# Two more steps with Q by seven half products, and the combinations they need made earlier

## The chip, the cores and the metric

The kernel runs on one core of a Trainium2 chip. The metric is the device time of one execution in microseconds, the median of several runs.

## The reference

A cross-attention layer with a gate, then a quantized linear layer with a gate. `x` and the context are (32, 64, 512); there are 32 heads in 8 groups of 4 that share K and V, and head size is 128.

```python
Q = (layernorm(x) @ Wq.T).reshape(b, s, 8, 4, 128)
K = (ctx @ Wk.T).reshape(b, s, 8, 128)
V = (ctx @ Wv.T).reshape(b, s, 8, 128)
scores = einsum('bqhed,bkhd->bheqk', Q, K) * 128 ** -0.5      # causal mask
probs = softmax(scores)
attn = einsum('bheqk,bkhd->bqhed', probs, V).reshape(b, s, 4096)
x = x + tanh(g_xattn) * (attn @ Wd.T)
x = x + tanh(g_ffn) * (layernorm(x) @ dequantized.T + bias)
```

## The kernel before, in words

**Numbers in two halves.** Every float32 operand of a large product is scaled by a power of two and written as a high and a low float16 part. ScalarE (ACT) writes the high part, VectorE (DVE) or GpSimd (POOL) the low one, and TensorE (PE) multiplies high by high, high by low and low by high (`PASSES`). So one product over 512 inputs of 512 columns is 12 matmuls, each 128x512.

**Steps.** The 2048 tokens are 4 blocks of 512. A step n handles one group of heads g = n % 8 of one block tb = n // 8, so there are 32 steps. In step n PE computes the scores of n, then Q, K and V of the next step m = n + 1, transposes the probabilities of n, multiplies them by V (`av_unit`), and adds the output product of n (`y_unit`, four units, one for each tile of 128 tokens, with the weight `wd`). The order on every engine is written out by hand, and semaphores tie the engines together. In block 0 the weights are read in float32, split and kept in DRAM (`kept_q`, `kept_k`, `kept_v`, `kept_d`); from block 1 on each step reads its split weights back (`back_qkv` at line 431, `back_d` at line 445), all from SyncE's queue (SP), which issues its DMAs strictly in the order of the program.

**Q by seven half products.** For a step m with `fast(m)` Q is not made by `q_unit` but by `run` (line 1741). For two heads at a time the product of weights and tokens is cut in two along the heads, the inputs and the tokens, and the eight quarter products are replaced by seven (Strassen's scheme in Winograd's form). A half product is 6 matmuls of 128x256; two pairs of heads make 14 of them, 84 matmuls, in place of 48 of 128x512. ACT copies partial results out of PSUM (`copy_p1`, `copy_p5`, `copy_u2`), DVE adds others to them, and both split the sums into the halves of q. Before the change `FIRST_FAST` is 24, so steps 24 to 31 are fast, all of block 3.

**What a fast step needs beforehand.** The sums of quarters of the weights ("mixed" weights) of each group, made once: `load_mix` reads a group's float32 weights into `raw_s` (half of `raw_d`), POOL combines them (`mix_weights`, four operations), ACT and DVE split them (`mix_hi`, `mix_lo`) into `ws`, and `keep_mix` writes them to `kept_s`. `MIX_STEPS` says in which steps this happens, one group each; `back_mix` reads them back for a fast step, issued two steps ahead. The tokens need combinations too: `mix_norm` makes them from the normalised block on POOL, with `mixed_hi` on ACT and `mixed_lo` on POOL, in the step with g = 4 of the block before (`mix_of`); `transpose_mixed` turns them by 32 DMA transposes into `tT`, which lies in `raw_q`, 16 each in two steps.

**Put-off output units.** When the step after next is fast (`deferred(n)` is `fast(n + 2)`), y units 2 and 3 of step n run in the middle of step n + 1. In a step whose successor is fast, `back_d(n)` waits for them, since they still read the buffer of `wd`, so `transpose_some` (line 499) issues it behind the first `FEW` = 5 of the step's transposes and not ahead of all of them:

```python
for one in some:
    ...
    if one is some[FEW - 1] and fast(n + 1) and n < LAST:
        back_d(n)
```

The norm of a block comes in step 3 of the block before, its transposes in the steps after it; in step 20 these are 18. Step 10 unpacks half of the FFN weight on DVE (`ffn_weight`) and takes the norm's statistics; step 11 has the FFN of block 0 among its matmuls.

Of the kernel before, what the change touches and what calls it, by code (L numbers as in the profile page):

```python
# [15 lines left out]
HEADS, GROUPS, DK = 32, 8, 128  # L16
HPG = HEADS // GROUPS
KC = D // P
# [37 lines left out]
def build(nc, x, ctxT, wqT, wkT, wvT, wdT, g_x, g_f, qw, w_scale, w_zero, bias, out):  # L56
    with ExitStack() as stack:
        def sb(name, shape, dt=F32):
            return stack.enter_context(nc.sbuf_tensor(name, shape, dt))
# [4 lines left out]
        def sem(name):  # L64
            return stack.enter_context(nc.semaphore(name))
# [11 lines left out]
        raw_q = sb("raw_q", [P, 2, HPG, KC, DK])  # L77
# [3 lines left out]
        raw_d = sb("raw_d", [P, 2, HPG, D])  # L81
# [5 lines left out]
        k = sb("k", [P, 2, BT], F16)  # L87
# [7 lines left out]


        tT = [raw[:, 0, :, :, :].rearrange("p h k n -> p (h k n)").bitcast(F16).rearrange(
            "p (c k n) -> p c k n", c=2, k=KC) for raw in (raw_q, raw_q)]
        ws = [raw[:, 1, :, :, :].rearrange("p h k n -> p (h k n)").bitcast(F16).rearrange(
            "p (c h k n) -> p c h k n", c=2, h=HPG, k=KC)  # L100
            for raw in (raw_q, raw_d.rearrange("p c h (k n) -> p c h k n", k=KC))]
# [63 lines left out]
        def pair(name):  # L165
            return [sem(name + "0"), sem(name + "1")]
# [5 lines left out]
        s_ld, s_kept, s_back = sem("s_ld"), pair("s_kept"), pair("s_back")  # L172
        s_mix, s_hi, s_lo = sem("s_mix"), sem("s_hi"), sem("s_lo")
# [18 lines left out]
        wq_hi, wq_lo = sem("wq_hi"), sem("wq_lo")  # L192
# [35 lines left out]
        def backs(m):  # L228

            return 16 * ((m - GROUPS) // 2 + 1)  # L230
# [71 lines left out]

        FIRST_FAST = 3 * GROUPS
        FIRST_BLOCK = FIRST_FAST // GROUPS
        RUN = ((0, 1), (0, 5), (0, 2), (0, 6), (0, 7), (0, 3), (1, 1), (1, 5), (1, 2), (1, 6), (1, 7), (1, 3))

        def fast(m):

            return FIRST_FAST <= m < STEPS

        def pair_count(m, r):

            return 2 * (m - FIRST_FAST) + r + 1

        def run_count(m, r, i):

            return len(RUN) * (m - FIRST_FAST) + RUN.index((r, i)) + 1

# [17 lines left out]
            return part.rearrange("p (b u s) -> p b u s", b=BPB // 2, u=HALVES)  # L338


        MIX_STEPS = (7, 12, 13, 14, 15, 17, 18, 21)
        MIX_ORDER = tuple((FIRST_FAST + i) % GROUPS for i in range(GROUPS))

        def mixing(n):

            return MIX_STEPS.index(n) if n in MIX_STEPS else None

# [38 lines left out]
        def _(sp):  # L386
# [101 lines left out]

            def transpose_mixed(tb, some):

                sp.wait_ge(wq_lo, HPG * GROUPS)
                for t, c, i in some:
                    sp.wait_ge(t_hi, TILES * (tb - FIRST_BLOCK) + t + 1)
                    sp.wait_ge(t_lo, TILES * (tb - FIRST_BLOCK) + t + 1)
                    sp.dma_start(tT[tb % 2][:, c, i, t * P:(t + 1) * P], th[:, t, c, i * P:(i + 1) * P],
                                 transpose=True).then_inc(t12_ld if t >= 2 else t3_ld if i < 2 else t4_ld, 16)


            def transpose_some(n):

                g, tb = n % GROUPS, n // GROUPS
                some = []
                if tb > 0 and g in (1, 2):
                    call = NORMS.index((2, tb - 1))
                    some = transposes(call)[16 * (g - 1):16 * g]
                elif 0 < tb < BLOCKS - 1 and g >= 4:
                    call = NORMS.index((1, tb + 1))
                    if fast(GROUPS * (tb + 1)):
                        if g == 4:
                            some = transposes(call)[EARLY:]  # L510
                        elif g < 7:
                            call, some = None, MIXED[16 * (g - 5):16 * (g - 4)]
                    elif g < 6:
                        some = transposes(call)[16 * (g - 4):16 * (g - 3)]
                    elif tb + 1 >= FIRST_BLOCK:
                        call, some = None, MIXED[16 * (g - 6):16 * (g - 5)]
                for one in some:
                    if call is None:
                        transpose_mixed(tb + 1, [one])
                    else:  # L520
                        transpose_norm(call, [one])
                    if one is some[FEW - 1] and fast(n + 1) and n < LAST:
                        back_d(n)
                if not some and fast(n + 1) and n < LAST:
                    back_d(n)
# [23 lines left out]
            def back_mix(m):  # L549

                sp.wait_ge(q_mm, 4 * (m - 1))
                sp.wait_ge(s_kept[m % 2], 16 * GROUPS // 2)
                sp.dma_start(ws[m % 2].rearrange("p c h k n -> p (c h k n)"), kept_s[m % GROUPS]).then_inc(s_back[m % 2], 16)

            def load_ffn():
# [36 lines left out]
            for n in range(STEPS):  # L592
                g, tb, m = n % GROUPS, n // GROUPS, n + 1
# [18 lines left out]
                if fast(m + 1):  # L612
                    back_mix(m + 1)
# [1094 lines left out]
        def _(pe):  # L1708
# [32 lines left out]
            def run(m, r, i):  # L1741
# [3 lines left out]
                if (r, i) == (0, 1):  # L1745
                    pe.wait_ge(q_back[m % 2], backs(m))
                    pe.wait_ge(s_back[m % 2], 16 * ((m - FIRST_FAST) // 2 + 1))
                    if m % GROUPS == 0:
# [417 lines left out]
```

## Time and profile before

| | us |
|---|---|
| median of 3 runs | 1046.54 (1046.34 to 1047.17) |
| profiled execution | 1045.23 |
| its span, first to last instruction | 1043.4 |
| PE busy | 1006.0 |
| DVE busy | 720.3 |
| ACT busy | 500.3 |
| POOL busy | 290.2 |
| mean granted clock of TensorE | 0.997 of 2.4 GHz |

Busy time is the union of an engine's instructions. The timeline gives instructions in order of time, with equal neighbours merged; a start is counted from the first instruction of the span. A step is taken to begin with the first matmul of its scores. Line numbers are those of the kernel before.

### The profile page before, as it was taken

The page shows a single profiled execution, that of the slowest core. Times are in us where ns is not written, and L with a number is a line of the kernel's source. Part 1 is how long each engine was busy: PE and PEld are TensorE (multiplying, and loading weights), DVE is VectorE, ACT ScalarE, POOL GpSimd, SP SyncE. Part 2 cuts the span into 40 slices and gives each one's busy share as a digit, 9 for nine tenths or more (in the row PEclk, how much of TensorE's full clock was granted, in tenths as well). Part 3 has the DMA queues.
Part 4 walks back from the last instruction along what each step waited for, and adds up shares of the span by engine and source line. Part 5 has one row for each costly group of instructions (what it writes and reads, how often), then busy time and mean ns, then how long its engine had stood idle before and what let it go on. Part 6 is the DMA issues. An engine that isn't in the chain of part 4 may idle for free.

```text
span 1043.4 us, 21305 instructions
## 1 busy us (share of the span) xinstructions
PE 1006.0 (96%) x8130; PEld 597.5 (57%) x8130; DVE 720.3 (69%) x1484; ACT 500.3 (48%) x1033; POOL 290.2 (28%) x287
## 2 busy tenths in 40 slices
PE   5889999999999999999999999999999999999996
PEld 3455555555555555455555555555567776767752
DVE  6856777777586676865667667565667767666678
ACT  5777676675633343334543434334444444444422
POOL 1355665465714001412210503143000120000004
PEclk9999999999999999999999999999999999999998
DMA  7748546534474542455544775146754444543211
GB/s 281 229 150 289 204 160 203 163 101 169 130 258 139 155 92 102 157 157 177 207 172 162 237 212 176 26 162 181 216 162 149 158 130 148 180 140 138 91 42 60
DMA packets 97523, 168.65 MB, mean 162 GB/s; under 512 B 35472, under 2 KB 68240, under 8 KB 83728
## 3 DMA queue, kind: packets, MB, share of 16 engines
q1 hardware_dynamic: 97424, 167.30, 49.6%
q8 instruction: 66, 1.08, 0.5%
q14 instruction: 33, 0.27, 0.1%
HBM read 110.89 MB, written 33.55 MB: 138 GB/s over the span
## 4 chain that ended last, share of the span: by engine, by line
PE 84%; DVE 10%; ACT 3%; issue 2%; DMA 1%; SPq 0%; DVEq 0%; ACTq 0%
PE pa L1715 33%; PE py L1715 30%; PE av L1894 5%; PE pa L1790 4%; PE av L1790 3%; PE pp L1872 3%; PE ps L1856 2%; PE pp L1856 2%; DVE q L1214 2%; PE py L1954 1%; DVE sc L1310 1%; DVE row_max L1308 1%; DVE sc L1304 1%; DVE sc L1321 1%; DMA raw_q<-in_wqT 1%
## 5 line engine op out<-in xcount | busy, mean ns | idle before, releaser
L1715 PE MATMUL py<-wd,att 128*128 128x512 f16 x1488 | 337.6, 379 | 1.7 <-DVE att L1334 0.9
L1715 PE MATMUL pa<-xT,wq 128*128 128x512 f16 x1152 | 257.2, 379 | 10.1 <-DVE q L1214 7.8
L1715 PEld LDWEIGHTS py<-wd,att 128*128 128x128 f16 x1488 | 143.1, 98 | 158.6 <-issue 2.8
L1715 PEld LDWEIGHTS pa<-xT,wq 128*128 128x128 f16 x1152 | 109.3, 98 | 145.2 <-issue 19.3
L1343 DVE SCALAR_TENSOR_TENSOR xacc<-py,f_y,xacc 128x512 f32<-128x512 f32 x128 | 95.7, 747 | 91.4 <-PE py L1715 91.3
L939 ACT ACTIVATE att<-av 128x256 f16<-128x256 f32 x256 | 80.8, 385 | 135.9 <-PE av L1894 135.4
L1334 DVE SCALAR_TENSOR_TENSOR att<-av,att 128x256 f16<-128x256 f32 x256 | 93.5, 418 | 65.6 <-ACT att L939 65.3
L888 ACT ACTIVATE q<-pa 128x512 f16<-128x512 f32 x96 | 56.7, 591 | 171.0 <-PE pa L1715 171.0
L1715 PE MATMUL pa<-wv,cT 128*128 128x128 f16 x1536 | 96.2, 219 | 0.0
L1715 PEld LDWEIGHTS pa<-wv,cT 128*128 128x128 f16 x1536 | 89.8, 98 | 0.9
L1214 DVE SCALAR_TENSOR_TENSOR q<-pa,q 128x512 f16<-128x512 f32 x96 | 65.8, 686 | 35.2 <-ACT q L888 33.5
L1715 PE MATMUL pa<-cT,wk 128*128 128x512 f16 x384 | 88.1, 379 | 1.6 <-DVE q L1214 1.4
L1894 PE MATMUL av<-pT,v_dup 128*128 128x256 f16 x512 | 71.6, 273 | 0.1
L680 POOL TENSOR_TENSOR xh<-xn,xh 128x512 f16<-128x512 f32 x28 | 33.8, 1234 | 124.0 <-ACT xh L912 124.0
L928 ACT CAST pr<-sc 128x256 f16<-128x256 f32 x64 | 32.7, 510 | 74.2 <-DVE sc L1321 74.1
L1214 DVE SCALAR_TENSOR_TENSOR k<-pa,k 128x512 f16<-128x512 f32 x32 | 22.1, 692 | 65.9 <-ACT k L894 65.9
L932 ACT COPY pT<-pp 128x1024 f16<-128x1024 f16 x64 | 64.3, 1005 | 4.7 <-PE pp L1872 4.2
L657 POOL TENSOR_SCALAR raw_d<-raw_d,w_mul 128x512 f32<-128x512 f32 x32 | 54.2, 1693 | 21.9 <-ACT wd L883 21.9
L1715 PEld LDWEIGHTS pa<-cT,wk 128*128 128x128 f16 x384 | 36.4, 98 | 41.7 <-issue 3.2
L747 POOL TENSOR_TENSOR xacc<-xacc,raw_kv 128x512 f32<-128x512 f32 x12 | 17.1, 1447 | 154.7 <-DVE raw_kv L1483 154.7
L1894 PEld LDWEIGHTS av<-pT,v_dup 128*128 128x128 f16 x512 | 48.2, 99 | 16.7 <-issue 0.3
L697 POOL TENSOR_TENSOR small<-rs 128x4 f32<-128x4 f32 x18 | 4.7, 262 | 168.4 <-DVE rs L1368 167.4
(180 smaller groups left out, 1396.8 us busy)
## 6 DMA issues: line engine op xcount, KB each, us to landing
wq<-kept_q SPq DMA_DIRECT2D x24, 1024.0 KB, 8.7
wd<-kept_d SPq DMA_DIRECT2D x23, 1024.0 KB, 6.8
v_dup<-v_nat SPq DMA_DIRECT2D x128, 128.0 KB, 2.4
raw_d<-in_wdT SPq DMA_DIRECT2D x8, 1024.0 KB, 10.3
kept_q<-wq SPq DMA_DIRECT2D x8, 1024.0 KB, 9.0
kept_d<-wd SPq DMA_DIRECT2D x8, 1024.0 KB, 5.6
raw_d<-in_wqT SPq DMA_DIRECT2D x8, 1024.0 KB, 7.1
raw_q<-in_wqT SPq DMA_DIRECT2D x7, 1024.0 KB, 5.5
```

Source lines behind the costliest of these rows:

```text
L657: pool.tensor_scalar(raw, raw, scale, None, ALU.mult).then_inc(w_scaled, 1)
L680: pool.tensor_tensor(xh[:, t % TILES, LO, :], xn[:, t % TILES, :], xh[:, t % TILES, HI, :], ALU.subtract).then_inc(x_lo, 1)
L888: act.activation(q[:, HI, :, :, h, :], pa[h % 2][:, :].rearrange("p (b u s) -> p b u s", b=BPB, u=HALVES), ACT.Copy, scale=Q_SCALE).then_i ...
L932: act.copy(pT[:, :, :, p * HQ:(p + 1) * HQ], pp[:, :].bitcast(F16).rearrange("p (b h s) -> p b h s", b=BPB, h=HPG)).then_inc(pT_ok, 1)
L939: last = act.activation(att[:, HI, :, at:at + S], av[j % 2][:, bb * 256:(bb + 1) * 256].rearrange("p (h s) -> p h s", h=HPG), ACT.Copy, sc ...
L1214: dve.scalar_tensor_tensor(out=out, in0=in0, scalar=scale, in1=hi, op0=ALU.mult, op1=ALU.subtract).then_inc(done, 1)
L1334: last = dve.scalar_tensor_tensor(out=att[:, LO, :, at:at + S], in0=av[j % 2][:, bb * 256:(bb + 1) * 256].rearrange("p (h s) -> p h s", h= ...
L1343: dve.scalar_tensor_tensor(out=acc(t), in0=py[j % 2][:, :], scalar=f_y[:, n:n + 1], in1=acc(t), op0=ALU.mult, op1=ALU.add).then_inc(y_ok, 1)
L1715: last = pe.matmul(out, stationary(a, i), moving(b, i), start=(i == 0 and (a, b) == PASSES[0]), stop=(i == count - 1 and (a, b) == PASSES[ ...
L1790: last = pe.matmul(half(bank), a[:, c, head, w_half + kc, :], b[:, d, b_half + kc, at], start=first and i in (1, 2, 5), stop=kc == 1 and ( ...
L1856: last = pe.matmul((pp, ps)[p][:, b * keys(p):(b + 1) * keys(p)], q[:, a, b, p, :, :].rearrange("p h s -> p (h s)"), k[:, c, b * S:b * S + ...
L1894: last = pe.matmul(av[j % 2][:, bb * 256:(bb + 1) * 256], v_dup[:, n % 2, b, c, :], pT[:, b, :, :].rearrange("p h s -> p (h s)"), start=(c ...
```

## The change

`FIRST_FAST` goes from 24 to 22. Steps 22 and 23, groups 6 and 7 of block 2, so get their Q by half products too, and their Q is made during steps 21 and 22. From this follow, by the rules above:

- `deferred` holds for steps 20 and 21 as well, and `fast(n + 1)` for n = 21 and 22: `back_d` of these two moves behind five transposes.
- `back_mix` of steps 22 and 23 is added to SP's queue, in steps 20 and 21, 1 MB each.
- `FIRST_BLOCK` becomes 2, so the combinations of block 2's tokens are made too: `mix_norm`, `mixed_hi` and `mixed_lo` in step 12, 32 more DMA transposes in steps 14 and 15.
- The order of the groups that are mixed begins with 6 and 7, and `MIX_STEPS` has 10 in place of 21. Step 12 mixes weights next to the norm's combinations. The first read of mixed weights waits for all of them.
- The transposed combinations of block 3 lie in `raw_d`, no longer in `raw_q`, and so wait for the last mixing of weights.

```diff
-            "p (c k n) -> p c k n", c=2, k=KC) for raw in (raw_q, raw_q)]
+            "p (c k n) -> p c k n", c=2, k=KC) for raw in (raw_q, raw_d.rearrange("p c h (k n) -> p c h k n", k=KC))]
...
-        FIRST_FAST = 3 * GROUPS
+        FIRST_FAST = 2 * GROUPS + 6
...
-        MIX_STEPS = (7, 12, 13, 14, 15, 17, 18, 21)
+        MIX_STEPS = (7, 10, 12, 13, 14, 15, 17, 18)
...
             def transpose_mixed(tb, some):
 
-                sp.wait_ge(wq_lo, HPG * GROUPS)
+                if tb == 2:
+                    sp.wait_ge(wq_lo, HPG * GROUPS)
+                else:
+                    sp.wait_ge(s_lo, HPG * GROUPS)
...
             def back_mix(m):
 
                 sp.wait_ge(q_mm, 4 * (m - 1))
-                sp.wait_ge(s_kept[m % 2], 16 * GROUPS // 2)
+                for par in range(2):
+                    sp.wait_ge(s_kept[par], 16 * GROUPS // 2)
```

SP's queue from the end of step 20 to step 21, before (`xT<-xh` are the norm's transposes, `raw_q<-raw_kv` those of the combinations, `raw_d<-in_wqT` the raw weights for the mixing of step 21):

```order
L486 DMA_TRANSPOSE xT<-xh 128x128 x18
L462 DMA v_dup<-v_nat 64x4x256 x4
L541 DMA raw_d<-in_wqT 128x2048
L449 DMA wd<-kept_d 128x4096
L436 DMA wq<-kept_q 128x4096
L440 DMA wk<-kept_k 128x1024
L443 DMA wv<-kept_v 128x1024
L495 DMA_TRANSPOSE raw_q<-raw_kv 128x128 x16
```

and now (`<-kept_s` are loads of mixed weights):

```order
L557 DMA raw_q<-kept_s 128x4096
L486 DMA_TRANSPOSE xT<-xh 128x128 x18
L462 DMA v_dup<-v_nat 64x4x256 x4
L436 DMA wq<-kept_q 128x4096
L440 DMA wk<-kept_k 128x1024
L443 DMA wv<-kept_v 128x1024
L557 DMA raw_d<-kept_s 128x4096
L498 DMA_TRANSPOSE raw_d<-raw_kv 128x128 x5
L449 DMA wd<-kept_d 128x4096
L498 DMA_TRANSPOSE raw_d<-raw_kv 128x128 x11
```

The load of wd has moved from ahead of wq's to behind five transposes; a load of mixed weights stands ahead of the 18 transposes and another ahead of the five.

PE at the end of step 20 and in the first part of step 21, before:

```order
L1715 MATMUL py<-wd,att 128x512 x12
L1894 MATMUL av<-pT,v_dup 128x256 x4
L1715 MATMUL py<-wd,att 128x512 x24
L1856 MATMUL pp<-k,q 128x32 x24
L1856 MATMUL ps<-k,q 128x64 x24
L1715 MATMUL pa<-xT,wq 128x512 x48
```

and now:

```order
L1719 MATMUL py<-wd,att 128x512 x12
L1898 MATMUL av<-pT,v_dup 128x256 x4
L1860 MATMUL pp<-k,q 128x32 x24
L1860 MATMUL ps<-k,q 128x64 x24
L1794 MATMUL pa<-xT,wq 128x256 x6
L1794 MATMUL pa<-raw_q 128x256 x6
L1794 MATMUL av<-xT,wq 128x256 x6
L1794 MATMUL pa<-raw_q 128x256 x6
L1719 MATMUL py<-wd,att 128x512 x12
```

Two y units (x24) have left the end of step 20; the first of them stands behind four half products of step 21.

## Rows read from the trace of the kernel before

**Rows 1.** The page, part 1: PE's busy time.
```profile
PE 1006.0 (96%) x8130; PEld 597.5 (57%) x8130; DVE 720.3 (69%) x1484; ACT 500.3 (48%) x1033; POOL 290.2 (28%) x287
```

**Rows 2.** Busy time by step (20 to 23, 25, 26): stretch, length, engines, clock, DMA.
```profile
677.62:708.21 30.59, 30.21 (x237) 16.95 (x236) 18.52 (x33) 11.73 (x24) 16.05 (x14) 1.00 0.45 143
708.21:738.48 30.27, 30.21 (x237) 16.93 (x236) 19.29 (x36) 14.54 (x28) 8.03 (x7) 1.00 0.56 160
738.48:763.58 25.10, 25.04 (x214) 14.60 (x213) 14.72 (x29) 11.44 (x22) 2.31 (x2) 1.00 0.76 226
763.58:792.44 28.86, 28.86 (x274) 20.52 (x272) 19.51 (x44) 12.46 (x30) 0.00 (x0) 1.00 0.54 175
...
821.63:850.50 28.87, 28.87 (x275) 20.54 (x273) 19.42 (x44) 14.90 (x38) 7.12 (x6) 1.00 0.42 143
850.50:880.33 29.83, 28.90 (x275) 20.53 (x273) 21.40 (x47) 12.46 (x30) 2.54 (x3) 1.00 0.52 160
```

**Rows 3.** Timeline of PE in step 25: start, length, engine, line, operation.
```profile
832.73 2.75 PE L1715 MATMUL py<-wd,att 128*128 128x512 f16 x12
...
844.45 2.75 PE L1715 MATMUL py<-wd,att 128*128 128x512 f16 x12
```

**Rows 4.** Timeline of SP's queue in steps 20 and 21.
```profile
688.24 23.23 SPq L486 DMA_TRANSPOSE xT<-xh  x18
711.57 2.60 SPq L462 DMA_DIRECT2D v_dup<-v_nat  x4
...
715.40 0.38 SPq L436 DMA_DIRECT2D wq<-kept_q  x1
...
717.18 22.11 SPq L495 DMA_TRANSPOSE raw_q<-raw_kv  x16
```

**Rows 5.** Timeline of SP's queue in step 26.
```profile
855.43 0.55 SPq L436 DMA_DIRECT2D wq<-kept_q  x1
...
857.04 0.59 SPq L553 DMA_DIRECT2D raw_q<-kept_s  x1
857.74 6.28 SPq L486 DMA_TRANSPOSE xT<-xh  x5
864.38 0.33 SPq L449 DMA_DIRECT2D wd<-kept_d  x1
```

**Rows 6.** Line L449, wd's loads: all 23, then that of step 26 alone.
```profile
DMA to landing us min/median/max: 4.7/6.8/10.1
...
DMA to landing us min/median/max: 7.2/7.2/7.2
```

**Rows 7.** Line L1471 in all; timelines of POOL, PE and DVE in step 12.
```profile
L1471 DVE SCALAR_TENSOR_TENSOR xacc<-ff_rows,small,xacc x16: 742/782/1748, 423.0 to 1037.5; 128x512 f32<-128x512 f32 x16
...
429.77 5.58 POOL L747 TENSOR_TENSOR xacc<-xacc,raw_kv 128x512 f32<-128x512 f32 x4
...
437.68 2.75 PE L1715 MATMUL pa<-xT,wq 128*128 128x512 f16 x12 [0.66 <-DVE q L1214]
...
455.05 1.41 DVE L1214 SCALAR_TENSOR_TENSOR raw_d<-raw_d,w_mul 128x512 f16<-128x512 f32 x2
```

**Rows 8.** Timeline of ACT at the end of step 20 and in step 23.
```profile
703.78 2.18 ACT L1000 ACTIVATE raw_kv<-xn 128x512 f16<-128x512 f32 x4
...
765.73 0.37 ACT L948 COPY p<-pa 128x256 f32<-128x256 f32 x1 [1.30 <-PE pa L1790]
```

**Rows 9.** Timelines of DVE and PE in step 11.
```profile
395.52 0.68 DVE L1214 SCALAR_TENSOR_TENSOR q<-pa,q 128x512 f16<-128x512 f32 x1
...
398.67 2.75 PE L1715 MATMUL pa<-xT,wq 128*128 128x512 f16 x12
```

**Rows 10.** PE's timeline in the tail, then a stretch of it with its granted clock.
```profile
1024.32 3.63 PE L1954 MATMUL py<-ff_w,xT 128*128 128x512 f16 x16 [0.66 <-ACT xT L919]
...
1030.88 5.31 PE L1954 MATMUL py<-ff_w,xT 128*128 128x512 f16 x16 [0.49 <-DVE xn L1483]
...
1031.20:1034.50 3.30, 3.30 (x10) 1.09 (x9) 3.27 (x5) 0.55 (x1) 3.30 (x3) 0.50 0.00 0
```

## The prediction, made before the run

> **What bounds the kernel now.** I read the page first: TensorE is busy 1006.0 of 1043.4 us, 96% [rows 1]. So I cut the span into steps at the first score matmul of each step and read busy times by step [rows 2]. Step 21 lasts 30.27 us with PE busy for 30.21, step 25, which makes its Q by half products, 28.87 with PE busy for all of it. Every other engine has at least 9 us left over in such a step. The rule that follows: a step takes what its matmuls take, and another engine or a transfer matters only where PE arrives and finds its operand missing. So the change is priced in two ways: matmuls removed, and new places where PE can arrive too early.
>
> **What it removes.** Steps 21 and 22 compute the Q of groups 6 and 7 of block 2. Each becomes a step like 25: 30.27 - 28.87 = 1.40 us less. Step 22 is short in the trace before (25.10) only because y units 2 and 3 of its output product are put off into step 23. Now step 20 puts off its two first, steps 21 and 22 hand two on and take two, step 23 is as it was. Steps 20 to 23 together go from 30.59 + 30.27 + 25.10 + 28.86 = 114.82 to 25.41 + 28.87 + 28.87 + 28.86 = 112.01. **Term 1: -2.8 us.** The important by-product: step 21 no longer starts at 708.21 but at 677.62 + 25.41 = 703.03, 5.2 us sooner, because its predecessor gave work away.
>
> **What it adds on the SP queue of step 21; this decides.** SP issues in order, and it is late there already: step 20's 18 transposes hold it from 688.24 to 711.57, then come four copies of V, then the loads of step 21 [rows 4]. None of this waits for PE, so it does not move up with PE. I write SP's new clock:
> - A load of mixed weights (1 MB) stands ahead of the 18 transposes. Such a load holds SP 0.6 us [rows 5]. The V copies end at 711.57 + 2.60 + 0.6 = 714.8.
> - The load of raw weights for the mixing of step 21 and wd's load go from here. The wq, wk, wv loads take 717.18 - 715.40 = 1.8, the second new load of mixed weights 0.7: 717.3.
> - Now the change's own order: wd's load stands behind five transposes, since its buffer is free only once the put-off y units have run. Five hold SP 22.11 / 16 x 5 = 6.9 [rows 4] or 6.3 [rows 5]. I take 6.6: wd is issued at 723.9.
> - wd lands 7.2 us after its issue in step 26, the nearest case, with the same loads and transposes ahead of it [rows 5, 6]: 731.1. Over all steps it is 4.7 to 10.1, median 6.8 [rows 6].
>
> When does PE want it? In step 25, y unit 0 starts 844.45 - 821.63 = 22.8 us into the step [rows 3], so at 703.03 + 22.8 = 725.8, or 726.1 with the small wait below. **Term 2: 731.1 - 726.1 = +5.0 us of PE standing still.** Bounds: five transposes at 6.3 and a landing in 4.7 give 2.2 us; 6.9 and 10.1 give 8.2. The buffer itself is no limit: the second put-off y unit starts 832.73 - 821.63 = 11.1 into the step [rows 3] and ends 2.7 later, at 717, while SP gets there at 723.9.
>
> In step 22 the same order is harmless. That step then starts near 737; SP is through with the 11 other transposes (15.2) and the V copies near 742, 5 us into the step, as in step 26 (850.50 to 880.33), where SP began its loads at 855.43 and wd, issued at 864.38, landed at 871.6, ahead of the 873.3 at which it was wanted [rows 2, 5, 6]. Term: 0, up to 1.
>
> **What the wait does to the clock.** The tail shows what an idle PE costs: after a stretch with waits the granted clock reads 0.50, the 1.2 GHz level, and the 16 matmuls that took 3.63 us at the full 2.4 GHz take 5.31 [rows 10], 1.68 more. I expect the clock to fall once during or after the 5 us; part of the slow stretch may fall into the wait itself, where it is free. Ends 0 and 1.7, I take 1.1. **Term 3: +1.1.** The Trainium skill (TensorE: Matmul & The Clock Gate, the section on HAM oscillation) says the same of PE gaps spent waiting for a DMA: it comes back at half rate. By its rule the term is nearer to the full 1.7 than to 0; nothing in the middle of this trace tests it, since PE never waits there for over 1 us.
>
> **Mixing of weights, moved from step 21 to step 10.** Step 21 had room for it. Step 10 has the tightest DVE: behind y unit 1 stand the norm's statistics and the unpacking of the FFN weight, and DVE does the first low part of q in step 11 only at 395.52 [rows 9]. Four low parts more are 2 x 1.32 = 2.6 us (two take 1.41, overlapping by a little [rows 7]), so that part moves to 398.2 and ends at 398.8. PE wants it at 398.67, after the first FFN tile. Step 11's FFN units give DVE its time back. **Term 4: +0.3**, between 0 and 1.5 (if the unpacked weight is late as well).
>
> **Norm's combinations in step 12.** POOL gets eight operations more, some 11 us at the 1.4 us that four of its additions took apiece [rows 7], right behind the mixing of weights, so beside DVE's four low parts. Where POOL's additions overlapped, one DVE operation on SBUF operands (L1471) took up to 1.75 us in place of 0.74, and PE lost 0.66 at its fourth Q unit of step 12 [rows 7]. The same can happen in step 13. **Term 5: +0.5**, between 0 and 1.5. The Trainium skill (GPSIMD Engine Reference, its quick facts) has POOL and DVE contend for one SBUF interface when DVE reads two SBUF tensors; the low parts are of that kind. By that rule all four stretch and the term is at its upper end; were there no such contention, it would be 0. The 32 new transposes of steps 14 and 15 take SP 22 of 30.27 us in each, as in steps 12 and 13, where nothing waited: 0, or a few tenths. ACT's new hi parts fill idle time.
>
> **Start of step 21.** ACT does the norm's hi parts for block 3 until 703.78 + 2.18 = 706.0. Nobody wanted ACT then; now step 21 needs its first copy, in step 23 made 2.15 us after the start (765.73) [rows 8], so at 705.2. It comes 0.8 later; PE uses it after a few half products more. DVE's scores meet POOL there too. **Term 6: +0.3**, between 0 and 1.
>
> **Sum:** -2.8 + 5.0 + 1.1 + 0.3 + 0.5 + 0.3 = +4.4. The profiled execution took 1045.23 us and would take 1049.6; the median of the runs is 1046.54, 1.3 above it, so I forecast **1050.9**.
>
> **Rivals.**
> - *A, wd's load comes in time.* The other side: faster. Place: SP in step 21. It decides at an issue before 726.1 - 7.2 = 718.9. For it: in steps 25 and 26 this very order costs nothing [rows 5, 6]. Against it: there SP was idle ahead of it, here it is 5 us behind from step 20. Also if transposes issue quicker with their sources long ready. Time: -2.8 + 0.8 on 1046.5, about 1044.7. Chance 0.13.
> - *B, a short wait, no loss of clock.* wd lands in 4.9 and SP is a little quicker: 2.5 us, small terms 0.8. Time 1047. Chance 0.2. For it: the loads of step 21 stand in a queue with fewer bytes, since raw weights and a write of mixed weights are gone.
> - *C, more than one wait.* SP's delay carries into step 22 (wd again) or DVE falls behind in steps 13 and 21 by their upper ends: 1054. Chance 0.12. For it: the wq, wk, wv and mixed loads pile up with 16 transposes. Against: the 5 us wait itself gives SP time.
> - *D, the change misses its aim:* half products that run where PE waits for DVE and save nothing. Steps 23 and 25 ran at 28.86 and 28.87 [rows 2], so I give this no chance of its own; step 26 (29.83) shows what a DVE with four operations more does, and that is inside C.
>
> **How the numbers follow.** The main case has 0.55: a wait of 4 to 6 us, with or without the clock, 1049 to 1053. The range takes in all of it, B, part of A and most of C: 1044.8 to 1054.5. A measurement of this kernel tells 0.2% (2.1 us) from nothing. Slower than that: the main case but its lower edge (0.53) and C (0.12), 0.65. Within: B and that edge, 0.23. Faster by more: A at its best, 0.12.
>
> **What would show it.** A PE wait of about 5 us ahead of y unit 0 of step 21, ended by the load of wd, which SP issued near 724 behind five transposes; a granted clock of 0.50 just after it. Steps 20 to 23 otherwise near 25.4, 28.9, 28.9, 28.9. A wait of some tenths at the third Q unit of step 11 and in step 13. I am wrong if wd's load of step 21 is issued before 719, or lands within 4 us, or if step 22 shows the larger wait. If the total comes out right with step 21 at 29 us, it was right by accident.

## The result, and the profile after

The changed kernel takes 1051.79 us in the median of five runs (1049.03 to 1054.55), the kernel before 1046.34 beside it. The ratio is 1.0050, 95% interval 1.0037 to 1.0064: **slower by 5.2 us, between 3.9 and 6.7**. A later series on another occasion gave 1.0044 (1.0030 to 1.0058). The profiled execution took 1051.79 too, its span is 1050.0.

Busy time by step in the profile after, steps 20 to 23 (answers to [rows 2]); the columns are the stretch, its length, then PE, PEld, DVE, ACT, POOL, the granted clock, DMA:

```profile
679.98:705.39 25.41, 25.04 (x213) 14.59 (x212) 16.48 (x30) 9.00 (x18) 12.32 (x10) 1.00 0.70 207
705.39:741.37 35.98, 31.28 (x275) 21.06 (x273) 19.58 (x43) 16.77 (x38) 7.50 (x6) 0.91 0.48 139
741.37:770.23 28.86, 28.86 (x274) 20.55 (x272) 18.91 (x43) 14.92 (x34) 2.32 (x2) 1.00 0.52 165
770.23:799.09 28.86, 28.86 (x274) 20.54 (x272) 19.49 (x44) 12.47 (x30) 0.00 (x0) 1.00 0.51 166
```

Three of the four are what the half products promise. Step 21 is 7.1 us too long, and it alone shows a clock below 1.00. Its place is in PE's timeline:

```profile
732.94 5.12 PE L1719 MATMUL py<-wd,att 128*128 128x512 f16 x12 [4.70 <-DMA wd<-kept_d]
...
738.34 2.75 PE L1719 MATMUL py<-wd,att 128*128 128x512 f16 x12
```

That is y unit 0 of step 21. PE stood for 4.70 us until the load of wd landed; then its 12 matmuls took 5.12 us, those of the next unit 2.75. SP's queue (answers to [rows 4, 5]):

```profile
690.90 24.34 SPq L486 DMA_TRANSPOSE xT<-xh  x18
715.34 2.60 SPq L462 DMA_DIRECT2D v_dup<-v_nat  x4
718.05 0.55 SPq L436 DMA_DIRECT2D wq<-kept_q  x1
...
719.67 0.58 SPq L557 DMA_DIRECT2D raw_d<-kept_s  x1
720.35 6.27 SPq L498 DMA_TRANSPOSE raw_d<-raw_kv  x5
726.72 0.53 SPq L449 DMA_DIRECT2D wd<-kept_d  x1
```

The load of wd was issued at 726.72, 21.3 us into the step, and landed 6.2 us later:

```profile
DMA to landing us min/median/max: 6.2/6.2/6.2
```

The granted clock around it, in two stretches of the same columns as above (answers to [rows 10]):

```profile
728.20:730.90 2.70, 0.04 (x1) 0.00 (x0) 1.10 (x3) 2.62 (x5) 0.73 (x1) 1.00 0.84 328
731.00:737.70 6.70, 4.76 (x12) 1.73 (x13) 0.00 (x0) 0.32 (x1) 1.48 (x2) 0.50 0.19 43
```

PE had been idle since 728.2; the clock fell to 0.50 (1.2 GHz) within the wait and stayed there until PE had worked 4.8 us again. By length, step 21 is 28.87 + 4.70 + 2.41, and the last number is the clock.

Steps 11 and 12 (answers to [rows 7, 9]) show the work that moved forward. They took 37.33 and 30.88 before:

```profile
392.83:430.48 37.65, 37.55 (x274) 20.38 (x273) 28.97 (x64) 11.85 (x24) 8.55 (x15) 1.00 0.33 113
430.48:461.06 30.58, 30.21 (x237) 16.96 (x236) 21.27 (x37) 14.17 (x28) 19.82 (x16) 1.00 0.53 172
```

The profiled spans differ by 6.6 us, steps 11, 12 and 20 to 23 by only 0.32 - 0.30 + 4.29 = 4.3. The rest lies ahead of step 0, in code that both kernels share: step 0 begins at 39.83 after and at 37.46 before. The same 12 matmuls of the first Q unit take 5.25 us in the one and 2.75 in the other, after and then before:

```profile
19.29 5.25 PE L1719 MATMUL pa<-xT,wq 128*128 128x512 f16 x12 [1.19 <-ACT xT L923]
```
```profile
19.42 2.75 PE L1715 MATMUL pa<-xT,wq 128*128 128x512 f16 x12 [1.33 <-ACT xT L919]
```

That is the pace of the low clock, but the granted clock of this stretch of the profile after reads 1.00:

```profile
10.00:24.30 14.30, 11.34 (x51) 6.48 (x52) 9.16 (x17) 9.29 (x14) 2.50 (x2) 1.00 0.80 312
```

So that it is the clock is not shown here. Three other profiles of this study (mixed_weights_early, two_moves, wd_after_three) have a first Q unit of 4.4 us, and in them the granted clock over that unit reads 0.60 to 0.61. Step 0 began between 37.0 and 39.8 us in the profiles of this study, whatever the kernel. The span of a single profile against another says nothing under about 3 us for that reason. Step lengths can be compared: where two profiles do the same work without waiting for wd they agree within 0.1 us. The length of a wait for a transfer differs from one execution to another, though, and two experiments below show it.

### The profile page after: what moved, and what is told of

Its sections match the earlier page's. It is cut to its first block, busy times and chain, and to the rows that moved or that the text cites. A ratio compares the mean times of both kernels' runs of the same rounds, so it can differ in the third digit from the quotient of the medians.

```text
span 1050.0 us, 21624 instructions
## 1 busy us (share of the span) xinstructions
PE 1008.3 (96%) x8202; PEld 606.2 (58%) x8202; DVE 725.4 (69%) x1504; ACT 507.8 (48%) x1057; POOL 303.0 (29%) x295
## 4 chain that ended last, share of the span: by engine, by line
PE 83%; DVE 10%; ACT 3%; issue 2%; SPq 1%; DMA 1%; DVEq 0%; ACTq 0%
PE pa L1719 31%; PE py L1719 30%; PE av L1898 5%; PE pa L1794 5%; PE av L1794 3%; PE pp L1876 3%; PE ps L1860 2%; PE pp L1860 2%; DVE q L1218 2%; PE py L1958 1%; DVE sc L1314 1%; DVE row_max L1312 1%; DVE sc L1308 1%; DVE sc L1325 1%; DMA raw_q<-in_wqT 1%
## 5 line engine op out<-in xcount | busy, mean ns | idle before, releaser
L1719 PE MATMUL pa<-xT,wq 128*128 128x512 f16 x1056 | 240.0, 384 | 9.6 <-DVE q L1218 7.5
L1719 PEld LDWEIGHTS pa<-xT,wq 128*128 128x128 f16 x1056 | 101.1, 99 | 136.6 <-issue 23.5
L892 ACT ACTIVATE q<-pa 128x512 f16<-128x512 f32 x88 | 52.0, 591 | 148.4 <-PE pa L1719 148.4
L1218 DVE SCALAR_TENSOR_TENSOR q<-pa,q 128x512 f16<-128x512 f32 x88 | 60.3, 685 | 27.4 <-ACT q L892 25.9
L713 POOL TENSOR_TENSOR raw_d<-raw_d 128x512 f32<-128x512 f32 x8 | 10.1, 1266 | 144.1 <-DVE k L1218 144.1
```

What stands on the lines that cost most here:

```text
L892: act.activation(q[:, HI, :, :, h, :], pa[h % 2][:, :].rearrange("p (b u s) -> p b u s", b=BPB, u=HALVES), ACT.Copy, scale=Q_SCALE).then_i ...
L1218: dve.scalar_tensor_tensor(out=out, in0=in0, scalar=scale, in1=hi, op0=ALU.mult, op1=ALU.subtract).then_inc(done, 1)
L1719: last = pe.matmul(out, stationary(a, i), moving(b, i), start=(i == 0 and (a, b) == PASSES[0]), stop=(i == count - 1 and (a, b) == PASSES[ ...
```

## The experiments

Each edits the changed kernel unless something else is said, and the diffs are cut to their main lines; what else is edited is said below them. "Into step 21" counts from the first score matmul of that step.

### Is it SP's order alone? wd ahead of the mixed weights

```diff
+                if n == 21:
+                    back_d(n)
                 if fast(m + 1):
                     back_mix(m + 1)
```

(The load at the fifth transpose is left out for step 21.)

> The changed kernel, but in step 21 the load of wd stands behind the loads of wq, wk and wv and ahead of the load of mixed weights and of all 16 transposes. My theory: the 4.7 us wait of the changed kernel is SP's order alone. The buffer is free 13.9 us into the step (two put-off y units), which is about when SP gets there, so wd is issued near 14 us into the step and, with only 1.5 MB ahead of it, lands within 7 us, before the 22.8 us at which PE wants it: no wait, no low granted clock, step 21 at 28.9 us and the kernel 2.8 us faster than the kernel before, near 1043.6. Rival (the put-off y units keep the buffer too long, whatever the order): a wait of over 2 us stays and the kernel is at 1046 or above.

Ratio 1.0030 (1.0017 to 1.0043). In step 21 the theory held: wd, issued 15.0 us into the step, landed 7.9 later, PE waited 0.1. But the wait is not gone. Steps 21 and 22:

```profile
703.09:732.15 29.06, 28.91 (x275) 20.45 (x273) 19.59 (x43) 16.78 (x38) 7.52 (x6) 1.00 0.64 167
732.20:767.53 35.33, 31.56 (x274) 21.19 (x272) 18.92 (x43) 14.91 (x34) 2.31 (x2) 0.90 0.49 140
```
The wait of step 22, in the view of who waited for whom (total, times, longest), and wd's issues in SP's timeline:

```profile
PE py L1721 <- DMA wd<-kept_d: 3.8, 1, 3.8
```
```profile
718.15 0.69 SPq L449 DMA_DIRECT2D wd<-kept_d  x1
752.89 0.53 SPq L449 DMA_DIRECT2D wd<-kept_d  x1
```

Step 22 now starts 6.9 us sooner than in the changed kernel, counted from the start of step 20, SP does not, and wd of step 22 goes out 20.7 us into its step behind five transposes. The put-off y units are not the limit (that rival falls), and the time of 1043.6 that I expected was wrong: I had removed the wait that gave SP its time back.

### The same, behind the mixed weights

```diff
+                if n == 21:
+                    back_d(n)
                 for one in some:
```

(The load at the fifth transpose is left out for step 21.)

> The changed kernel, but in step 21 the load of wd stands behind the load of mixed weights and ahead of all 16 transposes. If only the time at which SP issues it counts (6.4 us sooner than in the changed kernel), wd lands near 727 and the wait is gone, as in the run above. Rival: the megabyte of mixed weights just ahead of it fills the DMA engines until about 727.5 on the clock of the changed kernel, wd lands near 730 and PE waits 1 to 2 us, with or without a fall of the clock: 1045 to 1047.

Ratio 1.0005 (0.9996 to 1.0015). In the profiled execution the rival had the direction and was too mild: PE waited 4.58 us. The timelines of PE and SP, then the flight of this load:

```profile
730.56 4.45 PE L1721 MATMUL py<-wd,att 128*128 128x512 f16 x12 [4.58 <-DMA wd<-kept_d]
...
718.38 0.70 SPq L559 DMA_DIRECT2D raw_d<-kept_s  x1
719.18 0.40 SPq L449 DMA_DIRECT2D wd<-kept_d  x1
```
```profile
DMA to landing us min/median/max: 11.3/11.3/11.3
```

wd was issued 5.3 us sooner into the step than in the changed kernel, and landed at nearly the same 27.4 us. In this execution SP's order was not what held it. Step 21 in it:

```profile
703.13:738.31 35.18, 30.59 (x274) 20.89 (x272) 19.59 (x43) 16.77 (x38) 7.52 (x6) 0.95 0.55 141
```

The ratio says that most executions of this kernel did better than the profiled one. By its step lengths it loses 3.5 us to the kernel before; the ratio allows 1.6 at most and says 0.5, where the changed kernel loses 4.6 to 5.2. So the place of wd alone gave back over 4 us in the median and only 0.8 in the profiled step. How long wd flew in the other executions no trace shows. An estimate from the ratio: 2.8 us saved by the half products and 0.5 lost in all leave 3.3 us for waits and clock together, in place of 7.4 to 8.0 in the changed kernel. That fits the rival's wait of 1 to 2 us with a fall of the clock.

### Three transposes ahead of wd, and eight

```diff
-                    if one is some[FEW - 1] and fast(n + 1) and n < LAST:
+                    if one is some[(3 if n == 21 else FEW) - 1] and fast(n + 1) and n < LAST:
```

and 8 in place of 3.

> The changed kernel with three transposes, not five, ahead of the load of wd in step 21. Theory: every transpose taken from ahead of it makes the issue 1.28 us sooner, so the issue is 2.6 us sooner and the wait 4.7 - 2.6 = 2.1 us. Whether the granted clock falls after a wait of 2 us is open: without a fall step 21 takes 28.9 + 2.1 = 31.0 us and the kernel about 1046, with one 32 to 33 us and about 1048. Rival (the engines are full until mixed weights and transposes have landed, so the issue matters little): the wait stays above 3.5 us.

> The changed kernel with eight transposes ahead of the load of wd in step 21. Theory: the issue is 3 x 1.28 = 3.8 us later, the wait 8 to 8.5 us, and the stretch at the low clock costs about what it costs in the changed kernel (2.4 us), as its length does not grow with the wait: step 21 near 40 us and the kernel 3.5 to 4 us above the changed one, near 1055.5. If the low stretch did grow with the wait, 1057 or more.

y unit 0 of step 21 in PE's timeline, with three and with eight:

```profile
733.22 4.33 PE L1719 MATMUL py<-wd,att 128*128 128x512 f16 x12 [5.54 <-DMA wd<-kept_d]
```
```profile
735.26 5.16 PE L1719 MATMUL py<-wd,att 128*128 128x512 f16 x12 [9.75 <-DMA wd<-kept_d]
```

With three, the wait was 5.54 us and not 2.1 (ratio 1.0037, 1.0024 to 1.0050). With eight, wd was issued 27.4 us into the step and landed 5.2 later; the wait was 9.75, over the 8.5 expected. Step 21 took 41.05: 28.87 + 9.75 + 2.43. So the cost of the clock did not grow with the wait. Here too the profiled execution was not the typical one: by step lengths it loses 9.4 us, by the ratio 7.0 (1.0067, 1.0054 to 1.0080), some 2 us more than the changed kernel where 3.5 to 4 were expected. From zero to five transposes, wd lands at 27.4 to 28.4 in the profiles, whatever its place; with eight its place decides. Something ahead of the transposes holds it: the megabyte of mixed weights was the suspect.

### Mixed weights in step 19

```diff
-                if fast(m + 1):
+                if fast(m + 1) and m + 1 > 23:
                     back_mix(m + 1)
+                if n == 19:
+                    back_mix(22)
+                    back_mix(23)
```

(For these two loads `back_mix` no longer waits for the Q matmuls of the step before.)

> The changed kernel, but both new loads of mixed weights (2 MB) are issued in step 19, where the queue is idle; wd of step 21 keeps its place behind five transposes. The four runs before showed that an earlier issue of wd alone does not help while a load of mixed weights stands just ahead of it: issued 16.0, 19.8 and 21.3 us into step 21, it landed 27.4, 28.3 and 27.5 into it. New theory: bytes ahead of it in the queue hold it. Without the mixed weights wd is issued 1.3 us sooner (+20.0) and has only wq, wk, wv (1.5 MB) and five transposes ahead of it, all through by then, so it lands 5 us later, at +25: a wait of 2 to 2.5 us where there were 4.7, and step 21 between 31 and 33 us. If SP's order were all, the wait would be 4.7 - 1.3 = 3.4 us or more.

Ratio 1.0031 (1.0021 to 1.0042). The same unit:

```profile
731.57 4.11 PE L1722 MATMUL py<-wd,att 128*128 128x512 f16 x12 [4.00 <-DMA wd<-kept_d]
```

The wait fell to 4.00 only. wd went out at 20.8 and landed at 26.8. That the mixed weights were gone shortened wd's flight by 0.2 us alone, to 6.0: in the changed kernel they landed 8.2 us after their issue at 719.67, only 1.2 us after wd was issued, so behind five transposes little of them was still ahead. In the profiles neither "SP's order" nor "bytes ahead" is the cause by itself: take one away and the other holds wd nearly as long.

### Both at once

```diff
+                if n == 21:
+                    back_d(n)
                 for one in some:
```

on top of the edit above.

> The changed kernel with the two new loads of mixed weights in step 19 and wd of step 21 ahead of all transposes; stores and step 22 as in the changed kernel. It tells what the other two moves of four_moves gave. Bytes ahead in step 21 are those of four_moves, so wd lands near +24 and PE waits 1 to 1.5 us there; step 22 starts early and SP is behind, wd of step 22 is issued near +19 behind five transposes and PE waits 2 to 4 us, probably with a fall of the clock: the total at the kernel before or 1 to 3 us above. If the stores and the shorter row of transposes in step 22 gave nothing, it equals four_moves.

Step 21 is cured, 28.87 us, where a wait of 1 to 1.5 was expected: wd issued at 14.3, landed at 22.5, PE did not wait. Step 22 waits in its place (its busy times, then the waits):

```profile
734.20:767.70 33.50, 30.59 (x275) 20.93 (x273) 18.91 (x43) 14.92 (x34) 2.31 (x2) 0.95 0.50 147
```
```profile
PE py L1724 <- DMA wd<-kept_d: 2.9, 1, 2.9
```

Ratio 1.0014 (1.0001 to 1.0027).

### Four moves

```diff
-                if ffn_of(n) is not None:
-                    for t in range(ffn_of(n) * TILES, (ffn_of(n) + 1) * TILES):
+                if n == 11 or n == 23:
+                    for t in range((0 if n == 11 else 1) * TILES, (1 if n == 11 else 2) * TILES):
                         store(t)
...
-                    if one is some[FEW - 1] and fast(n + 1) and n < LAST:
+                    if one is some[(2 if n == 22 else FEW) - 1] and fast(n + 1) and n < LAST and n != 21:
```

on top of the two moves.

> The changed kernel with four moves on SP's queue: mixed weights of steps 22 and 23 loaded in step 19; the four stores of block 1, for which SP waits until 8 us into step 20, issued in step 23; wd of step 21 ahead of its transposes; wd of step 22 behind two, not five. If SP's lateness and the bytes ahead of wd are the whole loss, wd lands before 22.8 us into both steps, steps 20 to 23 take 25.4, 28.9, 28.9, 28.9 us, the granted clock stays full, and the kernel takes 2.5 to 2.8 us less than the kernel before: faster than both. Rival (moving loads only hands the wait on to step 22 or 23, as with wd ahead of the mixed weights, where step 22 waited 3.8 us): one of the steps 22 or 23 shows a wait over 1.5 us and the total is at or above the kernel before.

Ratio 0.9986 (0.9976 to 0.9995), the first below 1: 1.5 us gained where 2.5 to 2.8 were expected. Waits of 0.94 and 0.57 us remain, with the clock at 1.00 throughout:

```profile
704.71:734.57 29.86, 28.92 (x274) 20.47 (x272) 19.58 (x43) 16.78 (x38) 7.52 (x6) 1.00 0.55 127
734.57:764.05 29.48, 28.91 (x274) 20.52 (x272) 18.91 (x43) 14.91 (x34) 2.32 (x2) 1.00 0.51 164
```

wd took 9.9 and 8.7 us to land. Later stores made step 20 begin its transposes sooner, but its 18 took 27.26 us, where they took 24.34 in the changed kernel and 23.23 before, so SP came to the loads of step 21 hardly sooner: 12.2 us into it, 12.7 in the changed kernel.

### wd where few bytes are ahead

```diff
                              kept_q[g]).then_inc(q_back[par], 16)
+                if m == 23:
+                    back_d(21)
...
-                    if one is some[(2 if n == 22 else FEW) - 1] and fast(n + 1) and n < LAST and n != 21:
+                    if one is some[(1 if n == 22 else FEW) - 1] and fast(n + 1) and n < LAST and n != 21:
                         back_d(n)
+                        if n == 22:
+                            back_mix(24)
```

on top of four_moves, where `back_d(21)` at the transposes and the old place of `back_mix(24)` go.

> As four_moves, with wd's loads placed so that few bytes stand ahead of them: in step 21 between the loads of wq and wk, in step 22 behind one transpose and ahead of the mixed weights. In four_moves wd was issued 13.9 and 14.7 us into its steps and landed 9.9 and 8.7 us later, behind 2.5 MB, which left waits of 0.9 and 0.6 us. Theory (bytes ahead): with 1 MB ahead in step 21 and 1.5 MB mostly landed in step 22, wd lands 5 to 7 us after its issue, before 22.8: no wait in either, steps 20 to 23 at 25.4, 28.9, 28.9, 28.9 (112.1 in sum), 1.5 us less than four_moves and 2.7 less than the kernel before. Rival: the transposes issued behind wd are what slows it, and the waits stay above 0.5 us; or the transposes, now later, make step 23 wait.

**Ratio 0.9981 (0.9972 to 0.9989), median 1044.61 beside 1046.59: faster than both kernels.** Steps 20 to 23:

```profile
677.60:703.00 25.40, 25.02 (x213) 14.60 (x212) 16.47 (x30) 9.00 (x18) 12.32 (x10) 1.00 0.44 126
703.00:731.95 28.95, 28.92 (x275) 20.49 (x273) 19.61 (x43) 16.77 (x38) 7.52 (x6) 1.00 0.44 129
731.95:760.80 28.85, 28.85 (x274) 20.55 (x272) 18.91 (x43) 14.90 (x34) 2.32 (x2) 1.00 0.61 166
760.80:790.30 29.50, 29.07 (x276) 20.49 (x275) 19.56 (x44) 12.51 (x30) 0.00 (x0) 1.00 0.54 177
```
The one new wait that is left, and wd's issues:

```profile
PE pa L1801 <- DMA raw_d<-raw_kv: 0.4, 1, 0.4
```
```profile
716.90 0.33 SPq L451 DMA_DIRECT2D wd<-kept_d  x1
746.48 0.53 SPq L451 DMA_DIRECT2D wd<-kept_d  x1
```

wd landed 4.9 and 6.5 us after its issues, in time both times. What is left is what the rival's last clause said: transposes of step 22 are late for step 23, which waits 0.4 us and takes 0.6 more. The 2.0 us of the ratio stand beside the 2.2 of the step lengths; 2.7 were expected.

### One fast step fewer

```diff
-        FIRST_FAST = 2 * GROUPS + 6
+        FIRST_FAST = 2 * GROUPS + 7
```

> The changed kernel with FIRST_FAST at 23, so that only group 7 of block 2 gets Q by half products (in step 22). If the loss belongs to the first fast step while SP is behind, it moves there: step 22 starts near 733.3 on the clock of the kernel before, SP issues its wd near 751.5 behind the mixed weights and five transposes, it lands 6 to 8.5 us later, and PE waits 2 to 4 us and loses 1.5 to 2.7 us to the clock. Saved: 1.4. Sum: 2 to 5 us above the kernel before. If the loss were peculiar to step 21 (its queue, its norm), step 22 would take 28.9 and the kernel 1 us less than before.

Ratio 1.0049 (1.0033 to 1.0064), 5.1 us: just above the 2 to 5 expected, with half the gain and the same loss. y unit 0 of step 22, and the issue of its wd:

```profile
760.55 4.45 PE L1719 MATMUL py<-wd,att 128*128 128x512 f16 x12 [3.90 <-DMA wd<-kept_d]
...
754.47 0.53 SPq L449 DMA_DIRECT2D wd<-kept_d  x1
```

Step 21, put back, takes 25.09 us here and has no wait. The loss belongs to the first step whose predecessor has put off its y units, not to step 21. By step lengths this kernel loses only 4.2 us; what the rest of the 5.1 is stays inside the interval.

### The two pieces of work that moved forward, alone

```diff
-        MIX_STEPS = (7, 12, 13, 14, 15, 17, 18, 21)
+        MIX_STEPS = (7, 10, 12, 13, 14, 15, 17, 18)
```

on the kernel before,

> The kernel before with one edit: weights are mixed in step 10 and not in step 21. By my term 4 PE waits about 0.3 us more in step 11 and step 21 is as it was. If DVE's backlog did not reach PE, step 11 stays at 37.32 us; if the unpacked FFN weight were late too, it would be over 38.

and, also on the kernel before,

```diff
-        FIRST_BLOCK = FIRST_FAST // GROUPS
+        FIRST_BLOCK = 2
```

> The kernel before with one edit: the combinations of block 2's tokens are made (step 12) and transposed (steps 14 and 15), though nothing uses them. By my term 5 POOL's eight operations stretch DVE's low parts of mixed weights and step 13 waits 0.5 us (0 to 1.5). In the changed kernel step 13 took 30.27 us, so I now expect nothing: steps 12 to 15 within 0.05 us of the kernel before, DVE's four low parts perhaps longer but with time to spare. It also tells whether the 0.3 us that step 12 gained in the changed kernel came from here or from the order of the mixing.

Each ran once, so only step lengths are read. First the one (steps 11 and 12), then the other (steps 11, 12 and 13):

```profile
390.32:427.97 37.65, 37.55 (x273) 20.46 (x272) 29.00 (x64) 11.84 (x24) 8.52 (x15) 1.00 0.32 113
427.97:458.55 30.58, 30.21 (x237) 16.94 (x236) 21.04 (x37) 12.10 (x24) 12.32 (x10) 1.00 0.51 172
```
```profile
390.70:428.00 37.30, 37.30 (x273) 20.59 (x272) 26.85 (x61) 12.07 (x24) 7.15 (x15) 1.00 0.25 85
428.00:458.90 30.90, 30.23 (x238) 16.96 (x236) 21.82 (x37) 14.17 (x28) 20.13 (x16) 1.00 0.54 169
458.90:489.20 30.30, 30.24 (x237) 16.93 (x236) 20.61 (x37) 14.54 (x28) 10.37 (x9) 1.00 0.62 192
```

Mixing in step 10 costs 0.33 us in step 11 and gives 0.30 back in step 12, both as in the changed kernel; the net is nothing. The gain is in PE's wait for a low part of q at its fourth Q unit of step 12, 0.37 us in place of 0.66; why that part is ready sooner was not tried. The norm's combinations cost PE nothing in any step. DVE's timeline at the turn of step 12 to 13 shows what they do there (the first two rows are the four low parts of the mixed weights, the third an operation of the softmax; in the kernel before they take 1.41, 1.41 and 0.42):

```profile
455.33 1.41 DVE L1214 SCALAR_TENSOR_TENSOR raw_d<-raw_d,w_mul 128x512 f16<-128x512 f32 x2
...
457.32 2.55 DVE L1214 SCALAR_TENSOR_TENSOR raw_d<-raw_d,w_mul 128x512 f16<-128x512 f32 x2
...
461.41 0.87 DVE L1310 TENSOR_TENSOR sc<-sc,row_max 128x256 f32<-128x256 f32 x1
```

POOL makes the low halves of the combinations from 456.43 to 462.0. Beside it the last two low parts take 0.99 and 1.64 us in place of 0.75 each, and the softmax operation twice its time: 1.6 us in all, which fit into DVE's free time (its busy time in step 13 grows from 19.3 to 20.6). The first two low parts began before 456.43 and are not longer.

### The changed kernel again

> The changed kernel once more, on the chip of the runs beside it, for a tighter comparison and to see what its low stretch is in another execution: a wait of 4 to 6 us ahead of y unit 0 of step 21, a low stretch of 3.4 or 6.8 us that costs 1.6 to 2.7 us, the median 4 to 6 us above the kernel before. The steps outside 20 to 23 within 0.1 us of the first profile; what differs in the profiled spans beyond that lies ahead of step 0, where the clock rises sooner or later.

Nothing is edited. A wait of 5.21 us, step 21 at 35.98 again, so 1.90 for the clock. Ratio 1.0044.

```profile
731.93 4.62 PE L1719 MATMUL py<-wd,att 128*128 128x512 f16 x12 [5.21 <-DMA wd<-kept_d]
```

The steps outside 20 to 23 agree with the first profile to 0.03 us. The executions of the changed kernel spread over 1048.35 to 1054.55, those of the kernel before over 1044.71 to 1049.24 (but for one disturbed execution). The varying start of step 0 (38.20 us here, 39.83 in the first profile) is one part of that.

## Why the prediction was right, and where it was not

The forecast was 1050.9, range 1044.8 to 1054.5; measured 1051.79. Point by point:

- **Term 1, half products, -2.8 us.** Right: steps 20 and 23 at 25.41 and 28.86, step 22 at 28.86 for 28.87. The by-product, that step 21 starts 5.2 us sooner and SP does not follow, was the key to the case.
- **Term 2, the wait, +5.0.** 4.70 in one profile, 5.21 in the other, at the place and by the load named. The issue came 21.3 us into the step where 20.9 was worked out, the landing 6.2 later where 7.2 was taken. The number was right, its cause only a part of it. I took wd's flight as a constant and added it to the issue, and put rival A's point of decision at "an issue before 718.9". In wd_before_transposes wd was issued at 719.18, which would have left a wait of a few tenths; in the profiled execution its flight was 11.3 us and PE waited 4.58, and the ratio still leaves 3.3 us for wait and clock in the median. With the same weights ahead, an issue at 16.1, 19.8 or 21.3 us into the step ends at 27.4, 28.3 or 27.5 in the profiles. So SP's lateness and the bytes ahead both hold wd; how much each has differs between executions, and by the ratio an earlier place alone is worth over 4 us.
- **Step 22, term 0.** Right, with the reason given: the wait of step 21 gives SP its time. Three kernels show the other side: where step 21 waits under 1 us or not at all, step 22 waits 0.6 to 3.8 us. Only the kernel in which wd has few bytes ahead in both steps has neither.
- **Term 3, the clock, +1.1.** Too small: 2.41 and 1.90 in the two profiles of the changed kernel, 1.6 to 2.7 in all nine profiles of this study with a wait of 2.9 us or more. My upper end of 1.7, from the one slow stretch of the tail, was no upper end: the low level lasted over 6.7 us here. The Trainium skill (TensorE: Matmul & The Clock Gate, the section on HAM oscillation), which pointed to the upper end, agrees with this: every one of those nine waits for a DMA was followed by the low level, while waits of 0.94 and 0.57 us in four_moves were not. The prediction's remark that PE never waits over 1 us in the middle of the trace before was a misreading: PE waits 2.00 us for DVE ahead of 49.29 and 1.56 ahead of 243.71, and the matmuls right behind both run at full pace, 2.75 us for 12.
- **Term 4, mixing in step 10, +0.3.** 0.32 in step 11, most of it at the third Q unit, where the shifted low part was expected to hold PE, but 0.30 comes back in step 12, which I did not see.
- **Term 5, the norm's combinations, +0.5.** Wrong: 0. The step of the argument that failed is the price at PE: DVE loses some 1.6 us in steps 12 and 13, has the time for it, and PE does not wait. Two of the four low parts stretch, not all: the other two begin before those operations of POOL. The contention that the Trainium skill names (GPSIMD Engine Reference, section 1, Specifications: DVE instructions with two SBUF inputs contend with POOL) fits the two that stretch, 0.99 and 1.64 us in place of 0.75.
- **Term 6, start of step 21, +0.3.** 0: where wd is in time, step 21 takes 28.9 us.
- **Sum.** +4.4 forecast, +4.3 by the step lengths of the profile. The two errors, the clock 1.3 too small and terms 4 to 6 together 1.1 too large, cancel, and that is luck. The ratio gives 5.2 (3.9 to 6.7), and its difference from 4.3 lies within its interval. (Rival A's time is 0.2 us off its own sum: 1046.5 - 2.8 + 0.8 is 1044.5.)

So a faster TensorE part was more than given back by a transfer whose queue had been late all along and had not mattered, because PE was late there too.

## What to carry to other kernels

When a change makes the main engine reach a point sooner, go through every queue that does not move with it and compare the new time of need with the old time of arrival; here the queue's lateness was visible in the profile before, hidden by 5 us of work that was put off. A load that is late can be late for two reasons at once, its place in the queue and the bytes ahead of it. Moving one of them alone shortened this wait in the profiles by 1.2 us at most, where both together removed it; in the median of the executions the place alone gave back over 4 us, and still not all. (wd ahead of the mixed weights takes away both, and then step 22 waited.) So read what a wait is worth from a series of executions as well as from one trace. After curing one wait look at the next step before counting the gain, and add the low clock's cost to any wait of PE that is some microseconds long.

## What the runs showed of the hardware that I had not expected

- One 1 MB load (wd) took from 4.9 to 11.3 us to land in the same step of kernels that differ only in what is issued around it. Issued ahead of the transposes it took 4.9 with 1 MB of weights issued in the 3 us ahead of it, 7.9 to 9.9 with 1.5 MB, 11.3 with 2.5 MB, one profiled execution each; behind three to eight transposes it took 5.2 to 8.5.
- A wait of PE between 2.9 and 9.75 us costs 1.6 to 2.7 us more by the clock, with no visible dependence on its length.
- The beginning of step 0 moves by up to 2.8 us between executions of nearly the same code. In four of the fourteen profiles the first Q unit took 4.4 to 5.25 us in place of 2.75; three of them show a low granted clock there, the fourth does not.
- Freeing SP ahead of a row of DMA transposes need not bring the row's end forward as much: the 18 of step 20, begun 3.0 us sooner into the step than in the kernel before, took 27.3 us in place of 23.2. Why is open: in the kernel before the same 2.5 MB of loads stand ahead of the row, and stores besides.
